# Running the state recurrence by groups of four tokens, with gate and skip as columns of its matmuls

## The reference, cut to what matters

```python
# x: 8 batches x 512 tokens x 128 channels
x = x + 0.5 * moe(layernorm(x))        # 8 experts, top 1, at most 160 tokens for each
x = x + ssm(layernorm(x))
x = x + 0.5 * moe(layernorm(x))

def ssm(u):                            # per batch, in order of the tokens
    Bu = u @ B_w.T
    h_t = W h_(t-1) + Bu_t             # W is circulant and orthogonal: ifft(lambdas * fft(h))
    y_t = C_w h_t + D * u_t

def moe(u):                            # expert = argmax(u @ gate_w), place in it = running count
    out = prob * (relu(u_e @ w1[e]) @ w2[e])
```

## Time and profile before

| what | value |
|---|---|
| launch, median of 3 runs | 198.78 us (197.83 to 200.33) |
| profiled execution's own time | 196.14 us |
| its span | 194.3 us |
| PE busy | 156.8 us, 81% |
| DVE busy | 104.1 us, 54% |
| POOL busy | 87.4 us, 45% |
| ACT busy | 60.8 us, 31% |
| granted TensorE clock, mean of the span | 0.936 of full |

### The profile page before, as it was taken

One profiled execution on the slowest core, in us unless ns is written; L12 is line 12 of the kernel. 1 busy time (PEld: TensorE's weight loads), 2 busy tenths in 40 slices (PEclk: granted clock), 3 DMA queues, 4 the chain that ended last, 5 costly groups with the idle time before them and its releaser, 6 DMA issues. The chain is left out here.

```text
span 194.3 us, 2709 instructions
## 1 busy us (share of the span) xinstructions
PE 156.8 (81%) x882; PEld 111.4 (57%) x882; DVE 104.1 (54%) x341; ACT 60.8 (31%) x144; POOL 87.4 (45%) x90
## 2 busy tenths in 40 slices
PE   6899689997999896866679777786898875899930
PEld 3134456357989642326448645665895355798920
DVE  1043955512455404696796799999927134152230
ACT  3311241313643401762564453431100031363300
POOL 2400002773036550569777974973300477106472
PEclk9999995799999999999999999999559999699995
DMA  5999960111001118700212010110101011000110
GB/s 146 335 371 328 465 245 5 52 42 41 3 14 41 42 44 233 200 0 0 56 54 57 0 54 20 37 54 0 56 0 54 17 54 46 21 0 29 44 41 27
DMA packets 17309, 16.16 MB, mean 83 GB/s; under 512 B 1520, under 2 KB 14448, under 8 KB 17264
## 3 DMA queue, kind: packets, MB, share of 16 engines
q1 hardware_dynamic: 15648, 13.11, 22.2%
q0 software_dynamic: 1280, 2.62, 4.6%
q10 hardware_dynamic: 368, 0.26, 0.5%
HBM read 12.59 MB, written 5.51 MB: 93 GB/s over the span
## 5 line engine op out<-in xcount | busy, mean ns | idle before, releaser
L759 PE MATMUL bank<-warm_in,ones_bf 128*128 128x512 bf16 x121 | 31.2, 396 | 3.7 <-DMA x<-x_scratch 1.6
L878 PE MATMUL bank<-xcT,w1s 128*128 128x160 f32 x128 | 21.6, 310 | 3.0 <-issue 2.9
L759 PEld LDWEIGHTS bank<-warm_in,ones_bf 128*128 128x128 bf16 x121 | 11.3, 102 | 20.6 <-issue 7.4
L889 PE MATMUL bank<-hT,w2s 128*128 128x160 f32 x128 | 21.2, 312 | 1.7 <-issue 1.7
L292 POOL DMA_INDIRECT xg<-x,tok x10 | 10.2, 1020 | 27.2 <-DVE tok L601 24.4
L339 POOL TENSOR_TENSOR zs<-z,st 128x512 f32<-128x512 f32 x8 | 14.2, 1769 | 15.3 <-DVE z L731 15.3
L878 PEld LDWEIGHTS bank<-xcT,w1s 128*128 128x128 f32 x128 | 18.4, 193 | 4.5 <-issue 3.4
L889 PEld LDWEIGHTS bank<-hT,w2s 128*128 128x128 f32 x128 | 19.0, 199 | 2.4 <-issue 1.6
L397 ACT ACTIVATE hT<-bank 128x320 f32<-128x320 f32 x32 | 13.4, 435 | 21.5 <-PE bank L878 15.8
L947 PE MATMUL bank<-g,zc 128*128 128x128 f32 x56 | 11.3, 284 | 8.9 <-issue 6.1
L292 POOL DMA_INDIRECT xg<-out,tok x10 | 10.1, 1006 | 16.1 <-DVE tok L601 13.3
(11 more groups left out here) (154 smaller groups left out, 297.4 us busy)
## 6 DMA issues: line engine op xcount, KB each, us to landing
xt<-x_turned SPq DMA_DIRECT2D x8, 256.0 KB, 5.8
w1s<-w SPq DMA_DIRECT2D x2, 1024.0 KB, 8.6
w2s<-w SPq DMA_DIRECT2D x8, 256.0 KB, 7.3
x<-x_scratch SPq DMA_DIRECT2D x8, 256.0 KB, 5.1
out<-x SPq DMA_DIRECT2D x8, 256.0 KB, 2.3
cl<-const_late SPq DMA_DIRECT2D x1, 256.0 KB, 5.8
ce<-const_early ACTq DMA_DIRECT2D x1, 254.0 KB, 4.8
xg<-x,tok POOLq DMA_INDIRECT x10
```

What stands on the lines that cost most here:

```text
L759: M(bank[to][:, :], ones_bf[:, :], warm_in[:, :], start=True, stop=True)
L878: ins = M(bank[4 + half][:, c * CAP:(c + 1) * CAP], w1s[:, i, ch * P:(ch + 1) * P], xcT[:, i * CAP:(i + 1) * CAP], start=True, stop=True)
L889: ins = M(bank[6 + i % 2][:, 0:CAP], w2s[:, i, c, :], hT[:, i % 2, c, :], start=(c == 0), stop=(c == FC - 1))
```

## The change

The layout of tokens is new: partition p now holds the four tokens 4p to 4p + 3 of a batch, so a tile is every fourth token (`tiles`, the host's `x_turned` and `token_code` follow). A group of four tokens is then one partition index. With lag matrices `bk` (input weights turned by 0 to 3 steps) PE sums the four tokens of a group into one input of 128 columns; DVE turns it, scans over 128 groups and turns it forth; the sign and half swap of the complex product is a matmul with the permutation `turn`. The state carried into a group, `s_in`, is multiplied by four output tables `gall`, and the tokens inside a group act on each other by the products `kall` of 136 columns. `own` (144 columns) is a token's action on itself: lag 0, the skip D as a diagonal, its gate image, and 8 columns of the plain gate, which DVE multiplies by the standard deviation to get the logits of x itself. The turning of the output, its copy and its gate matmuls are gone, and so is all of POOL's work in the loop. The pieces of the second routing are 4, 3 and 1 batches, and `rank` counts in the new order. All of bk, gall, kall, bkT and own are made at run time: bk and gall on DVE behind the first index, the rest by `lag_tables` on PE and five copies on ACT behind the first expert stage.

```diff
-    PIECES = [[(0, NB)], [(0, 2), (2, 6), (6, NB)]]
+    PIECES = [[(0, NB)], [(0, 4), (4, NB - 1), (NB - 1, NB)]]
...
+            return rows[b * SEQ:(b + 1) * SEQ, :].rearrange("(p c) d -> p c d", c=TB)
...
+            nc.scalar.copy(bwT[:, :], bank[6][:, 0:P]).then_inc(tables, 1)
             act.wait_ge(set_ps, 2)
+            nc.scalar.copy(gT[:, :], bank[4][:, 0:2 * P])
+            nc.scalar.copy(bwc[:, :], bank[6][:, P:2 * P]).then_inc(tables, 1)
             act.wait_ge(set_ps, 3)
+            nc.scalar.copy(g1[:, D:PITCH], bank[4][:, 0:E])
+            nc.scalar.copy(g2[:, D:PITCH], bank[4][:, E:2 * E])
+            nc.scalar.copy(bk[:, 0, :], bank[6][:, 0:D])
+            nc.scalar.copy(bq[:, :], bank[6][:, D:2 * D]).then_inc(tables, 1)
...
+            act.wait_ge(fin_ps, 1)
+            nc.scalar.copy(bkT[:, :, :], bank[0].rearrange("p (k n) -> p k n", k=TB))
+            nc.scalar.copy(kall[:, 0:2 * PITCH], bank[1][:, 0:2 * PITCH])
+            nc.scalar.copy(kall[:, 2 * PITCH:4 * PITCH], bank[6][:, 0:2 * PITCH])
+            nc.scalar.copy(own[:, 0:PITCH], bank[1][:, 0:PITCH])
+            nc.scalar.copy(own[:, PITCH:OWN], gate_c[:, 0:E]).then_inc(fin_sb, 1)
...
+            deviation(0)
+            normalise(0)
+            copy_uT(0)
+            deviation(1)
+            normalise(1)
+            deviation(2)
+            for i in range(NB):
                 if i + 2 < NB:
...
+                if i + 1 < NB:
+                    copy_uT(i + 1)
+                copy_s(i)
+                if i + 3 < NB:
+                    deviation(i + 3)
...
+            def turned_tables():
+                dve.wait_ge(d_dcol, 16)
+                V.tensor_scalar(skip[:, 0:D], ident, dcol[:, 0:1], None, ALU.mult)
+                V.tensor_scalar(skip[:, D:PITCH], gate_c[:, 0:E], dcol[:, 0:1], None, ALU.mult).then_inc(skip_set, 1)
+                dve.wait_ge(tables, 3)
+                for k in range(1, TB):
+                    link(V.tensor_scalar(turned[:, 0:D], bq[:, :], st[:, k:k + 1], None, ALU.mult))
+                    link(V.scalar_tensor_tensor(bk[:, k, :], bk[:, 0, :], ct[:, k:k + 1], turned[:, 0:D],
+                                                ALU.mult, ALU.subtract))
+                    link(V.tensor_scalar(turned[:, :], g2[:, :], st[:, k:k + 1], None, ALU.mult))
+                    ins = V.scalar_tensor_tensor(gall[:, TB - 1 - k, :], g1, ct[:, k:k + 1], turned[:, :],
+                                                 ALU.mult, ALU.subtract)
+                    if k + 1 < TB:
+                        link(ins)
+                ins.then_inc(rows_set, 1)
...
+            group_tables()
+            turned_tables()
             slots(0)
...
+            def turn_back(b):
+                dve.wait_ge(b_ps, b + 1)
+                if b >= 1:
+                    dve.wait_ge(j_ps, b)
+                V.tensor_tensor(vb[:, :], bank[1][:, 0:P], s4[:, 0:P], ALU.mult).then_inc(vb_r, 1)
+                V.tensor_tensor(va[:, :], bank[1][:, 0:P], c4[:, 0:P], ALU.mult).then_inc(va_r, 1)
+            def run(b):
+                dve.wait_ge(va_r, b + 1)
+                dve.wait_ge(j_ps, b + 1)
+                V.tensor_tensor_scan(z[:, 1:P + 1], va[:, :], bank[1][:, P:2 * P], 0.0, ALU.add, ALU.add).then_inc(z_r, 1)
+                dve.wait_ge(z_r, b + 1)
                 if b >= 2:
+                    dve.wait_ge(s_ps, b - 1)
+                V.tensor_tensor(zs[:, b % 2, :], z[:, 0:P], s4n[:, :], ALU.mult).then_inc(zs_r, 1)
+                V.tensor_tensor(zc[:, b % 2, :], z[:, 0:P], c4[:, 0:P], ALU.mult).then_inc(zc_r, 1)
+            def rate_rows(b):
+                dve.wait_ge(y_ps, b + 1)
+                link(V.tensor_tensor(by_half(lg_own[:, :, :]), y_out(b)[:, :, :, PITCH:OWN],
+                                     by_half(ssd[:, b, :].unsqueeze(2).broadcast_to([P, TB, E])), ALU.mult))
+                V.tensor_tensor(by_half(logits2[:, b * TB:(b + 1) * TB, :]), y_out(b)[:, :, :, D:PITCH],
+                                by_half(lg_own[:, :, :]), ALU.add).then_inc(lg2_r, 1)
 
             def add_back(b):
 
+                V.tensor_tensor(by_half(x2[:, b * TB:(b + 1) * TB, :]), y_out(b)[:, :, :, 0:D],
+                                by_half(x1[:, b * TB:(b + 1) * TB, :]), ALU.add).then_inc(x2_r, 1)
+            stats(0)
+            invert(0)
+            stats(1)
+            invert(1)
+            stats(2)
+            for i in range(NB):
+                turn_back(i)
                 if i + 2 < NB:
+                    invert(i + 2)
                 if i >= 1:
+                    rate_rows(i - 1)
                     add_back(i - 1)
+                if i == ROUTE_FROM + 2:
+                    read_rank(1, 0)
+                run(i)
+                if i + 3 < NB:
+                    stats(i + 3)
                 if i == ROUTE_FROM:
...
+            mark(1, 1)
+            rate_rows(NB - 1)
+            mark(1, 2)
+            add_back(NB - 1)
+            read_rank(1, 1)
             make_hot(1, 1)
+            read_rank(1, 2)
...
+                q = rank_in(n, nb * TB)
...
+                M(q, ident_bf[:, :], counted[n][k][:, :, :], start=(k == 0), stop=False)
+                ends = counted[n][k][:, :, TB - 1::TB].unsqueeze(3).broadcast_to([P, E, nb, TB])
+                by_batch = q.rearrange("p e (b c) -> p e b c", c=TB)
+                if nb > 1:
+                    M(by_batch[:, :, 1:nb, :], above_bf[:, :], ends[:, :, 0:nb - 1, :], start=False, stop=False)
+                ins = M(by_batch, under_bf[:, :], ends, start=False, stop=True)
+                ins.then_inc(ranked, 1)
...
+            M(bank[6][:, P:2 * P], bwT[:, :], center[:, :], start=True, stop=True)
...
+            M(bank[6][:, 0:D], basis_in[:, 0:P], bwc[:, :], start=True, stop=True)
+            M(bank[6][:, D:2 * D], basis_in[:, P:2 * P], bwc[:, :], start=True, stop=True)
...
+            def lag_tables():
+                pe.wait_ge(row_sb, NS)
+                pe.wait_ge(rows_set, 1)
+                pe.wait_ge(skip_set, 1)
+                for k in range(TB):
+                    nc.tensor.transpose(bank[0][:, k * P:(k + 1) * P], bk[:, k, :], ident)
+                for m in range(TB):
+                    k_out = bank[1 + 5 * (m // 2)][:, (m % 2) * PITCH:(m % 2 + 1) * PITCH]
+                    ins = M(k_out, bk[:, m, :], g1, start=True, stop=(m > 0))
+                    if m == 0:
+                        M(k_out, center[:, :], skip[:, :], start=False, stop=True)
+                ins.then_inc(fin_ps, 1)
...
+            def group_sum(b):
+                pe.wait_ge(uT_sb, b + 1)
+                if b >= 1:
+                    pe.wait_ge(z_r, b)
+                for c in range(TB):
+                    ins = M(bank[1][:, 0:P], bkT[:, TB - 1 - c, :], uT_of(b, c), start=(c == 0), stop=(c == TB - 1))
+                ins.then_inc(b_ps, 1)
+            def own_rows(b):
+                if b >= 2:
+                    pe.wait_ge(x2_r, b - 1)
+                for c in range(TB):
+                    M(y_out(b)[:, c // 2, c % 2, :], uT_of(b, c), own[:, :], start=(c % 2 == 0), stop=False)
+            def turn_sum(b):
+                pe.wait_ge(vb_r, b + 1)
+                pe.wait_ge(va_r, b + 1)
+                M(bank[1][:, P:2 * P], turn, vb[:, :], start=True, stop=True).then_inc(j_ps, 1)
+            def cross_rows(b):
+                y = y_out(b)
+                def lags(m0, m1):
+                    return kall[:, m0 * PITCH:(m1 + 1) * PITCH].rearrange("p (m k) -> p m k", k=PITCH)
+                M(y[:, 0, 1, 0:PITCH], uT_of(b, 0), lags(1, 1)[:, 0, :], start=False, stop=False)
+                M(y[:, 1, :, 0:PITCH], uT_of(b, 0), lags(2, 3), start=False, stop=False)
+                M(y[:, 1, :, 0:PITCH], uT_of(b, 1), lags(1, 2), start=False, stop=False)
+                M(y[:, 1, 1, 0:PITCH], uT_of(b, 2), lags(1, 1)[:, 0, :], start=False, stop=False)
+            def state_in(b):
+                pe.wait_ge(zs_r, b + 1)
                 pe.wait_ge(zc_r, b + 1)
                 if b >= 1:
+                    pe.wait_ge(s_sb, b)
+                if b == ROUTE_FROM + 2:
+                    pe.wait_ge(rank_read, piece(1, 0) + 1)
+                M(bank[2][:, 0:P], turn, zs[:, b % 2, :], start=True, stop=False)
+                M(bank[2][:, 0:P], ident, zc[:, b % 2, :], start=False, stop=True).then_inc(s_ps, 1)
+            def state_rows(b):
+                pe.wait_ge(s_sb, b + 1)
+                y = y_out(b)
+                M(y[:, 0, :, 0:PITCH], s_in[:, b % 2, :], gall[:, 0:2, :], start=False, stop=True)
+                M(y[:, 1, :, 0:PITCH], s_in[:, b % 2, :], gall[:, 2:4, :], start=False, stop=True).then_inc(y_ps, 1)
+            lag_tables()
+            keep_warm(20)
+            pe.wait_ge(fin_sb, 1)
             pe.wait_ge(d_x1[0], 16)
             keep_warm(15)
             turn_u(0)
             keep_warm(2)
             for i in range(NB):
+                group_sum(i)
```

(46 more changed lines are left out.)

367 lines of the change are left out of this document (119 added, 248 removed).

## The result

The changed kernel took **184.43 us** in the median of 4 runs (184.25 to 188.35), the kernel before 198.31 (196.84 to 200.33) beside it; the ratio is 0.932 (0.926 to 0.938). Forecast: 184.8.

What follows compares the result with a forecast made beforehand. The prediction took a chain (scan, POOL's `zs`, read-out, `add_back`) to bound the kernel. 15.3 us less from loop to list plus 1.3 for setup made -14.0, so 184.8 us; own range 181 to 188.5, with the exchange rival 180.5 to 191.5.

Steps and rivals of the forecast that it cites:

- Pass 5.35 set by PE: New steady loop pass: PE's matmuls and transposes sum to 5.35 us and set it, against 6.69 before.
- the rival at 200.0: Matmuls writing two 136-column runs with a gap cost double, 1.9 us more a pass, 200.0 us in all; chance 6%.
- 0.35 spare before `state_in`: New pass: `zs` and `zc` end at 4.55 us, PE needs them at 4.9 behind `cross_rows`, so 0.35 is spare.
- exchange sets the pass: Rival: late DVE-PE handovers or DVE's list set the pass at 6.1 us, 190.8 in all; chance 19%.
- The read-out in the old pass: Old 6.69 us pass: the scan doesn't need the read-out, but DVE's order puts `add_back` ahead of the next scan.
- Seven passes 37.8: Loop: six passes 32.1 us, and a seventh of 5.7 that also holds `rank(1, 0)`.
- From there to `place(1, 1)` 12.2: Eighth pass to `turn_sum` 3.05 us, scan with `zs` and `zc` 1.0, then DVE alone 8.15.
- PE's end 6.35: Tail: `place(1, 1)` 1.4 us, eight dummies at half clock 3.45, 4 tiles 0.5, index 1.0.
- Loop to list 15.3 less: Loop's first matmul to the second token list: 56.35 us against 71.7, so 15.3 less.
- Setup +1.3: Extra PE matmuls and ACT copies before `place(0, 0)` make the first list 1.3 us late, bounds 0 to 3.
- the setup rival: Clock lost under `center_w1`, or tables beyond their cover, costs 3 us more, 187.8 in all; chance 8%.
- Tables 10.8 us ending at 43.9, cost 0: DVE's tables in setup take 10.8 us to 43.9, hidden under the wait for `eoT` with 2 us of cover.

Runs made afterwards that it cites:

- dve_more: Changed kernel with one unused 512-column DVE operation behind `add_back`, ahead of the scan, in each pass from the second on: 179.18 us, with 189.92 for the kernel before beside it.
- before_scan_first: Kernel before, with `add_back` of the previous batch issued behind the scan and `zc` in DVE's list: 214.05 us, 202.63 unedited beside it.
- No_dummies: Changed kernel without the eight dummy matmuls between `place(1, 1)` and `place(1, 2)`: 174.04 us, with 189.92 for the kernel before beside it.
- changed_third: Changed kernel run again without any edit, in the third job: 176.32 us, with 192.20 for the kernel before beside it.
- no_dummies_again: Second run, in the third job, of the changed kernel without the eight dummies between the last two places: 173.12 us, unedited changed kernel 176.32.
- Tables_late: Changed kernel with `group_tables` moved from ahead of the first expert stage to behind it: 178.93 us, with 189.92 for the kernel before beside it.
- before_zs_on_dve: Kernel before, with `zs` moved from POOL to DVE ahead of `zc`: 193.31 us, 192.20 unedited beside it, ratio 1.025.

## Why the prediction was right, point by point

- **The total, 184.8 against 184.43: nearer than it had a right to be.** By the loop (16.5) and the setup (0.85) of the profile it should have been 15.6 less and not 14.0; the medians are 13.9 apart. What took back the rest isn't shown, but the expert stages scatter by more than that. In the first and third job the changed kernel's median was 16.3 and 15.9 below the kernel before. So the mechanism was right, and a miss of only 0.4 us was luck. (The range's upper end also adds up to 189.1 and not 188.5; nothing hangs on it.)
- **Pass 5.35 set by PE: right, 5.29.** Dummies on PE lengthen it by their own time (0.42 of 0.43). The 272-column matmuls start 0.47 apart, 1.73 ns a column, as those without a gap. The Trainium skill ("PSUM — Partial Sum Buffer", Specifications) says that any non-contiguous pattern slows matmuls significantly; on these runs of 136 columns the trace doesn't agree, and the rival at 200.0 is out.
- **0.35 spare before `state_in`: wrong, 0.09.** The scan started 3.72 behind `group_sum`, not 3.55, because `own_rows`, `turn_u` and `turn_sum` end there; `zc` ended at 4.67, not 4.55, and PE was ready at 4.84, not 4.9: that is 0.17 by these, less the handover to PE of about 0.1. The forecast survived by a tenth of a microsecond; the rival "exchange sets the pass" was nearer than its 19% for a pass of 6.1 suggests, though dve_more shows that DVE's room in front of the scan is real.
- **The read-out in the old pass: half right.** "DVE's order ties them" left out that PE's order (`turn_x2` ahead of the next input) and POOL's list (`w` ahead of the next `vb`, which released the scan in before_scan_first) tie it as well. It also read the time in front of the scan as work, where `snb` was standing beside POOL. Undoing DVE's order alone cost 11 us. The forecast didn't lean on it, since the new pass was built up from its own columns.
- **Seven passes 37.8: 36.49** (84.19 to 120.68). The first has no `state_rows` and took 4.52; I had charged it in full. **From there to `place(1, 1)` 12.2: 12.17. PE's end 6.35: 6.53** (132.85 to 139.38), the dummies at half clock (0.50 from 130 to 139) and on the path, as forecast. No_dummies took out 3.2.
- **Loop to list 15.3 less: 16.5**, 1.2 more: 0.8 from the first pass, the rest from 0.06 in the others and a cheaper `rank` in the seventh.
- **Setup +1.3: +0.85** in this profile, not told to better than 1 us: the same kernel had its first list at 32.35, 33.60 and 34.02 us, the kernel before and its two edited versions at 31.50, 32.81 and 30.96. In the profile of changed_third the clock was half in this part (0.55 mean from 33.33 to 39.90) and the eight `center_w1` behind the place took 6.64 us; in that of no_dummies_again, the same instructions:

```profile
29.70 3.70 PE L838 MATMUL bank<-hot_tok,hot_place 128*64 128x20 f16 x32
33.33 6.64 PE L809 MATMUL bank<-w1s,center 128*128 128x512 f32 x8
```

```profile
27.73 3.70 PE L838 MATMUL bank<-hot_tok,hot_place 128*64 128x20 f16 x32
31.36 3.79 PE L809 MATMUL bank<-w1s,center 128*128 128x512 f32 x8
```

  So the setup rival's 3 us come and go between executions of one kernel; they did not make the verdict. The three lie within the bounds of 0 to 3. Tables_late, whose setup is the same, does not: in its profile the clock was 0.57 from 20 to 26 us and its first list came at 35.72, 4.2 behind the first profile of the kernel before. The kernel before can lose clock there too (0.70 from 22 to 27 us in before_scan_first), so the rival's loss is real and was bounded too low, but nothing shows that the change brings it.
- **Tables 10.8 us ending at 43.9, cost 0: right.** They ended at 43.83, and moving 6.8 us of them away changed nothing (first list to loop 44.43 both times).
- **What stays open.** In this profile ACT idled 5.83 us in the first expert stage and PE 3.61, with nothing that the profile shows outstanding:

```profile
44.56 0.51 PE L858 MATMUL bank<-gate_c,xcT 128*128 128x8 f32 x4
...
47.22 0.33 DVE L648 COPY eoT<-bank 128x160 f32<-128x160 f32 x1 [1.39 <-remote]
...
47.93 0.27 ACT L359 COPY xcT<-bank 128x128 f32<-128x128 f32 x1 [5.83 <-remote]
...
48.68 2.47 PE L869 MATMUL bank<-xcT,w1s 128*128 128x160 f32 x8 [3.61 <-ACT hT L367]
```

  The releaser given is "remote", another core or an unknown queue. The kernel runs on one core. Idle time with this releaser (2.4 to 6.0 us) stands in this stage of this profile and of all four of the first job, the kernel before with its scan first among them, and in none of the eight of the second and third job. The first profile of the kernel before has none in this stage, but 0.93 us in the second expert stage. So it looks to go with the chip or the hour rather than with the change; no run here tells its cause.

## What to carry to other kernels

Build the new steady state from columns and operations per engine, then compare the two longest ways; when they come within 0.3 us of each other, say so, for neither cover is safe. Before crediting a reorder or a move off an engine, look at what its neighbours will then overlap with. And dummies that keep the clock belong where the other engine still has work: the same eight moved from cover onto the path when the tail behind them became short.

## What the hardware showed that I had not expected

- **A scan beside POOL takes 2.2 to 2.3 us in place of 1.21**, in both edits of the kernel before. In before_zs_on_dve POOL's `w` runs from 99.56 to 100.84, the scan starts at 99.65 and is 1.06 longer than alone, nearly the 1.19 of the overlap. Read so, the scan waits for POOL's whole operation and then runs. The kernel before has it once itself, in its first batch:

```profile
84.28 1.27 POOL L316 TENSOR_TENSOR ud<-u,dsk 128x512 f32<-128x512 f32 x1
...
84.42 2.20 DVE L731 TENSOR_TENSOR_SCAN z<-va,vb 128x512 f32<-128x512 f32 x1
```

  In its steady pass `snb` stands there instead (0.74 in place of 0.16), and once it is the other way round: `zs` on POOL took 1.77, against 1.27 for POOL's other operations of that size, beside DVE's `zc`, which had started 0.04 earlier. DVE's `va`, which reads one input from PSUM, took 0.66 beside POOL's `w` (101.83), so it was not held up. The Trainium skill ("SBUF — State Buffer", "SBUF: two separate sides") describes this as an exclusive lock between the two engines: when DVE reads two SBUF inputs and POOL reads SBUF, whichever starts first holds it for its whole instruction. These numbers agree.
- **`place` takes nearly the same time at either clock**: 12 matmuls of 20 columns took 1.50 us in the changed kernel's tail at 0.50, 0.125 each, and 32 took 3.70 in no_dummies_again at 1.00, 0.116 each. Dummies ahead of `place` that only hold the clock for it gain next to nothing.
